# One stage's routing weights brought to the partitions by DMA instead of by matmul

## The reference, cut to what matters

```python
logits = jnp.einsum('bsd,de->bse', xn, Wr) + br
top_vals, top_idx = jax.lax.top_k(logits, K)                 # K = 2 of E = 8
w = jax.nn.softmax(top_vals, axis=-1)
w_full = jnp.einsum('bsk,bske->bse', w, jax.nn.one_hot(top_idx, E, dtype=w.dtype))
for e in range(E):
    h = jax.nn.gelu(jnp.einsum('bsd,dh->bsh', xn, W1[e]) + b1[e], approximate=False)   # H = 128
    y_e = jnp.einsum('bsh,hd->bsd', h, W2[e]) + b2[e]
    y = y + y_e * w_full[..., e, None]
```

## Time and profile before

| | |
|---|---|
| median of 3 runs | 560.65 us (560.37 to 564.43) |
| the profiled execution | 558.65 us |
| its span, first to last instruction | 556.9 us |
| TensorE busy | 515.6 us, 93% |
| VectorE busy | 458.4 us, 82% |
| ScalarE busy | 353.8 us, 64% |
| GpSimd busy | 80.0 us, 14% |
| expert units | from 464.9 us to the end |

### The profile page before, as it was taken

The page is one execution under the profiler, slowest core; times in us unless marked ns, Lnnn a source line. Parts: engine busy times, 40 slices in busy tenths (PEclk is TensorE's granted clock), DMA queues, the critical chain, the costliest instruction groups (busy, mean ns, idle before and its releaser), DMA issues.

```text
span 556.9 us, 12956 instructions
## 1 busy us (share of the span) xinstructions
PE 515.6 (93%) x4238; PEld 176.7 (32%) x4238; DVE 458.4 (82%) x540; ACT 353.8 (64%) x625; POOL 80.0 (14%) x180
## 2 busy tenths in 40 slices
PE   7999898557999999999999999999999888999996
PEld 6233332221333333333333333333333343233221
DVE  2668687778999999999999999999999786766644
ACT  2011222323889889898898898988988766445442
POOL 9601010203010010100100101001000451111000
PEclk9999999865999999999999999999999999999999
DMA  7910369373233232232332322323234101000000
GB/s 267 237 33 2 89 197 258 86 212 97 56 88 80 58 93 76 74 82 65 86 80 60 87 74 82 78 61 89 77 96 113 53 11 32 22 9 12 19 20 19
DMA packets 51095, 46.33 MB, mean 83 GB/s; under 512 B 26265, under 2 KB 39034, under 8 KB 51066
## 3 DMA queue, kind: packets, MB, share of 16 engines
q1 hardware_dynamic: 51066, 45.94, 30.5%
HBM read 29.75 MB, written 16.17 MB: 82 GB/s over the span
## 4 chain that ended last, share of the span: by engine, by line
PE 67%; DVE 5%; issue 1%; DMA 1%; ACT 1%; SPq 1%; POOL 0%; DVEq 0%; ACTq 0%; POOLq 0%
PE ps L1400 24%; PE ps L1312 13%; PE ps L1385 13%; PE ps L1533 5%; PE ps L1559 5%; DVE nmax L869 2%; PE ps L1326 1%; PE ps L1389 1%; DVE probs L1144 1%; PE ps L1546 1%; SPq L408 1%; PE ps L1450 1%; DMA maxima<-max_t 1%; PE ps L1556 1%; PE ps L1437 0%
## 5 line engine op out<-in xcount | busy, mean ns | idle before, releaser
L869 DVE TENSOR_REDUCE nmax<-ps 128x1 f32<-128x1024 f32 x256 | 301.6, 1218 | 18.7 <-PE ps L1312 9.9
L724 ACT ACTIVATE probs<-ps 128x512 f32<-128x512 f32 x512 | 278.1, 596 | 56.0 <-PE ps L1385 46.0
L1400 PE MATMUL ps<-probs,v_ring 128*32 128x256 f32 x2048 | 164.1, 393 | 0.0
L1312 PE MATMUL ps<-k_ring,q_ring 48*128 48x512 bf16 x512 | 102.9, 399 | 6.9 <-DVE nmax L869 6.9
L1385 PE MATMUL ps<-q_ring,k_ring 51*128 51x512 bf16 x512 | 101.3, 384 | 5.9 <-DMA q_ring<-maxima 1.7
L1312 PEld LDWEIGHTS ps<-k_ring,q_ring 48*128 48x128 bf16 x512 | 24.8, 93 | 113.7 <-issue 98.8
L1400 PEld LDWEIGHTS ps<-probs,v_ring 128*32 128x32 f32 x2048 | 40.5, 108 | 61.7 <-issue 36.8
L1144 DVE TENSOR_TENSOR probs<-probs,ps 128x1024 f32<-128x1024 f32 x32 | 39.0, 1220 | 25.4 <-PE ps L1546 20.1
L743 ACT ACTIVATE probs<-ps,wide_w 128x1024 f32<-128x1024 f32 x32 | 35.3, 1114 | 35.0 <-PE ps L1533 33.2
L890 DVE SCALAR_TENSOR_TENSOR gated<-ps,v_s,gamma_sb 128x1024 f32<-128x1024 f32 x32 | 40.7, 1280 | 10.9 <-PE ps L1234 10.7
L577 POOL TENSOR_TENSOR max_p<-nmax,zeros 128x8 bf16<-128x8 f32 x32 | 6.5, 202 | 282.4 <-DVE nmax L869 259.3
(11 more groups left out here) (162 smaller groups left out, 327.6 us busy)
## 6 DMA issues: line engine op xcount, KB each, us to landing
k_ring<-qk_parts SPq DMA_DIRECT2D x64, 96.0 KB, 2.4
q_ring<-qk_parts SPq DMA_DIRECT2D x64, 96.0 KB, 2.4
gamma_sb<-gamma_t SPq DMA_DIRECT2D x4, 1024.0 KB, 10.2
v_padded<-v_pad SPq DMA_DIRECT2D x4, 1024.0 KB, 5.0
v_ring<-v_padded SPq DMA_DIRECT2D x32, 128.0 KB, 3.2
outputs<-o_t SPq DMA_DIRECT2D x32, 128.0 KB
qk_parts<-qk_h SPq DMA_DIRECT2D x8, 384.0 KB, 4.3
x_ring<-bias_parts SPq DMA_DIRECT2D x32, 96.0 KB, 3.1
```

The lines of the kernel that those rows point to most:

```text
L724: A.activation(probs[:, s % 4, HALF * j:HALF * (j + 1)], ps[:, key_bank(s, j), :], ACT.Exp).then_inc(exp_done[j], 1)
L869: V.tensor_reduce(nmax[:, par, s:s + 1], ps[:, bank:bank + 2, :].rearrange("p a n -> p (a n)"), AX, ALU.max, negate=True).then_inc(s1_redu ...
L1312: return mm(ps[:, bank + j, :], q_ring[rows, u, P * s:P * (s + 1)], k_ring[rows, u, HALF * j:HALF * (j + 1)], start=True, stop=(s > 0 or j ...
L1400: last = mm(ps[VC * j:VC * (j + 1), PVB, 0:2 * P], v_ring[:, u, m, :], probs[:, m % 4, 2 * P * j:2 * P * (j + 1)], start=(m == 0), stop=(m ...
```

## The change

The weights of the units in `SENT` are no longer spread by TensorE. `SENT` is every unit k with k % 4 not zero and k above 2: units 3, 5, 6, 7, 9, 10, 11, 13 and so on to 31. That makes 22 of the 32 units as the code stands (24 have k % 4 not zero; units 1 and 2 are left out).

VectorE turns each batch's `w_full` in blocks of 32 x 32 (`weight_rows`, one transpose of 128 x 64 fp32 for each batch). SyncE stores the result in a DRAM tensor as one row of 128 weights for each tile and expert (`store_weights`: four DMAs a batch, of 64 runs of 128 bytes each). For each sent unit it loads them, the same four rows to each of the 128 partitions (`load_weights`: two DMAs, each 128 x 4 runs of 512 bytes, 256 KB, together 512 KB), into one of two buffers `w_wide`. The load into a buffer waits until the multiplication two sent units earlier has read it. The multiplication of a sent unit takes `w_wide` instead of the PSUM banks, and no longer waits for `spread`.

```diff
+    SENT = tuple(k for k in range(UNITS) if k % (E // 2) and k > 2)
...
+    w_scratch = nc.dram_tensor("weight_rows", [B, NT * E, P], fp32).ap()
...
+        w_rows = sb("w_rows", [P, B, NT * E], fp32)
+        w_wide = gated
...
+            def store_weights(b):
+
+                sp.wait_ge(w_rows_ready, b + 1)
+                for q in range(4):
+                    rows = slice(VC * q, VC * (q + 1))
+                    sp.dma_start(w_scratch[b, :, rows].rearrange("(h r) t -> r h t", h=2),
+                                 w_rows[rows, b, :].rearrange("r (h t) -> r h t", h=2)).then_inc(w_stored[b], 16)
+
+            def load_weights(k):
+
+                i, b, e = SENT.index(k), k // E, k % E
+                if i >= 2:
+                    sp.wait_ge(hid_scaled, SENT[i - 2] + 1)
+                sp.wait_ge(w_stored[b], 16 * 4)
+                for j in range(2):
+                    of = w_scratch[b, E * j + e, :]
+                    sp.dma_start(w_wide[:, i % 2, HALF * j:HALF * (j + 1)].rearrange("p (c n) -> p c n", n=P),
+                                 bass.AP(tensor=of.tensor, offset=of.offset, ap=[[0, P], [2 * E * P, NT // 2], [1, P]])
+                                 ).then_inc(w_loaded[i % 2], 16)
+
+            store_weights(0)
             store_output(G // RING + 1, (RING - 1) % 2, G - 1, RING - 1)
             for i in range(2):
                 sp.wait_ge(o_stored[i], 16 * G // 2 + 1)
             load_sums(B - 1)
+            for k in SENT[0:2]:
+                load_weights(k)
             store_inverse(B - 1)
             load_inverse(B - 1)
...
+            for k in SENT[2:]:
+                if k == E + 1:
+                    for b in range(1, B - 1):
+                        store_weights(b)
+                load_weights(k)
+                if k == 2 * E + 3:
+                    store_weights(B - 1)
+                if k > E and k % E == 5:
+                    store_result(k // E - 1)
+            store_result(B - 1)
...
+            def weight_rows(b):
+                V.transpose(w_rows[:, b, :], w_full[:, NT * b:NT * (b + 1), :].rearrange("p m e -> p (m e)")
+                            ).then_inc(w_rows_ready, 1)
...
-                               (weights_copy, 0), (first_choice, 1), (second_top, 1)):
+                               (weight_rows, 0), (weights_copy, 0), (first_choice, 1), (second_top, 1)):
...
-            WITHIN = {0: [(second_choice, 1)], 2: [(invert_sums, B - 1)], 4: [(two_weights, 1)], 5: [(all_weights, 1)],
+            WITHIN = {0: [(second_choice, 1)], 2: [(invert_sums, B - 1)], 4: [(two_weights, 1)], 5: [(all_weights, 1), (weight_rows, 1), (weight_rows, 2)],
...
-                dve.wait_ge(spread_done, k + 1)
                 if k >= 2:
                     dve.wait_ge(down_done, k - 1)
-                V.tensor_tensor(hid_w[:, k % 2, :], hid[:, k % 2, :],
-                                ps[:, 4:6, :].rearrange("p a n -> p (a n)"), ALU.mult).then_inc(hid_scaled, 1)
+                if k in SENT:
+                    i = SENT.index(k)
+                    dve.wait_ge(w_loaded[i % 2], 16 * 2 * (i // 2 + 1))
+                    weights = w_wide[:, i % 2, :]
+                else:
+                    dve.wait_ge(spread_done, spread_before(k) + 1)
+                    weights = ps[:, 4:6, :].rearrange("p a n -> p (a n)")
+                V.tensor_tensor(hid_w[:, k % 2, :], hid[:, k % 2, :], weights, ALU.mult).then_inc(hid_scaled, 1)
...
-                    pe.wait_ge(hid_scaled, k)
+                    pe.wait_ge(hid_scaled, max(n for n in range(k) if n not in SENT) + 1)
...
-                spread(k)
+                if k not in SENT:
+                    spread(k)
```

More of the change, by code:

```diff
@@ L288, in vit_tower_kernel @@
         y_seq = sem("y_seq")
+        w_rows_ready = sem("w_rows_ready")
+        w_stored = [sem(f"w_stored{b}") for b in range(B)]
+        w_loaded = [sem(f"w_loaded{i}") for i in range(2)]
         out_stored = [sem(f"out_stored{i}") for i in range(2)]
@@ L311, in up_bank, with spread_before @@
             return 0 if k % 2 else 2
+        def spread_before(k):
+            return k - sum(n < k for n in SENT)
         block = ctx.enter_context(nc.Block())
@@ L482, in _, with store_result @@
             load_sums(B - 1)
+            for k in SENT[0:2]:
+                load_weights(k)
             store_inverse(B - 1)
             load_inverse(B - 1)
-            for b in range(B):
+            def store_result(b):
                 halves = 2 if b == B - 1 else 1
@@ L1131, in residual @@
                 V.tensor_tensor(out_h, ye_v, h_v, ALU.add).then_inc(out_ready, 1)
-            WITHIN = {0: [(second_choice, 1)], 2: [(invert_sums, B - 1)], 4: [(two_weights, 1)], 5: [(all_weights, 1)],
+            WITHIN = {0: [(second_choice, 1)], 2: [(invert_sums, B - 1)], 4: [(two_weights, 1)], 5: [(all_weights, 1), (weight_rows, 1), (weight_rows, 2)],
                       6: [(route_parts, 1)], E: [(add_residual, B - 1), (center, B - 1)], E + 1: [(variance, B - 1)],
                       E + 2: [(scale, B - 1)], E + 6: [(logits_bias, B - 1), (first_choice, 2)],
-                      E + 7: [(second_top, 2), (second_choice, 2)], 2 * E + 1: [(two_weights, 2), (all_weights, 2)],
+                      E + 7: [(second_top, 2), (second_choice, 2)], 2 * E + 1: [(two_weights, 2), (all_weights, 2), (weight_rows, B - 1)],
                       2 * E + 2: [(route_parts, 2)]}
```

## The result

| | before | changed |
|---|---|---|
| median | 562.54 us (4 runs) | 617.99 us (4 runs, 613.66 to 620.43) |
| span of the profiled execution | 556.9 us | 615.1 us |
| first multiplication to end of span | 87.7 us | 142.7 us |

The ratio is 1.097, with a 95% interval of 1.092 to 1.103: the change made the kernel 9.7% slower. Nearly all of it arises in the expert units. The first multiplication (VectorE's product of `hid` and the weights, unit 0) starts at 469.25 us before and at 472.38 us after; from there to the end it is 556.9 - 469.25 = 87.7 us before and 615.1 - 472.38 = 142.7 us after, 55.1 of the 58.2 us by which the spans differ.

The account below looks back on a forecast made before the run. TensorE, full in the expert units, was taken as the bound: -0.4 - 3.96 - 0.6 + 0.3 = -4.66, say -4.6 us, from a median of 560.65 to 556.0 us; full range 554.0 to 577 us.

Parts of the forecast that it names:

- The bound, and the price of a pair: Expert units: TensorE is full, and each removed pair of spreading matmuls gives its queue back 0.22 us, 22 pairs 4.84 us.
- Transposes and stores: Four VectorE transposes at 0.25 us each, up to 0.5, and the stores on SyncE: hidden, at double price 0.5 us more.
- The cover of the sums: Sums, loaded later behind the first stores, land at 473.5 us; VectorE uses them at 475.18 us: 1.7 us of cover.
- The loads in steady state: Expert units: a load's data take up to 2.65 us, within the 2.83 us allowed; two buffers fit with nothing over.
- rival A: Loads run at the pace of `x_ring`, 264 packets a microsecond, 3.9 us each: 574.8 us on the median; chance 0.32.
- The first load: Unit 3's load, issued at about 473.4 us behind sums and outputs, expected at 477.6 us: cost 0.3 us.
- SyncE's queue: After the new stores, behind the first loads' four issues ending by 475.9 us, later transfers keep their cover: cost 0.
- It hardly moves: The store of the inverse sums, behind the issues of the first two loads on SyncE, was to stay nearly in place.
- Rival B: The round trip of the two buffers binds: at 5.0 us from multiplication's end to landing, 562.7 us; chance 0.15.
- The clock: Granted clock stays 1.00; if slow loads give TensorE gaps, it may be granted at the lower level, adding time.
- The range: 554.0 to 577 us, including slow loads at 3.9 us each; their slower half, chance some 0.16, stays outside.

Follow-up runs that it names:

- pairs_only: Changed kernel without transposes, stores or loads of weights, so the 22 pairs of spreading matmuls are gone with nothing in their place: 557.63 us, 0.994 of the kernel before.
- early_loads: rows2k_4buf with the load of unit 6 also issued ahead of the store and load of the inverse sums: 560.04 us, 0.994 of the kernel before.
- no_loads: Changed kernel with its transposes and stores but without the loads of weights and the waits for them: 559.42 us, 0.996 of the kernel before.
- same_4buf: Changed kernel with four buffers for the spread weights instead of two: 597.04 us, 1.061 of the kernel before.
- distinct: Changed kernel with each partition loading rows of its own from the input mixing matrix, same runs and buffers: 565.87 us, 1.003 of the kernel before.
- spaced: Changed kernel with transpose columns reordered and weights stored so a load's four shared rows lie 1 KB apart: 572.78 us, 1.019 of the kernel before.
- rows2k_4buf: rows2k with four buffers, one DMA a load and the first load issued before the wait for the last head's output: 563.15 us, 1.001 of the kernel before.
- copies: rows2k with each batch's rows stored 16 times, each eight partitions reading a copy of their own: 572.94 us, 1.017 of the kernel before.
- rows2k: Changed kernel with columns ordered before the transpose, so a load's four rows are one run of 2 KB: 568.62 us, 1.013 of the kernel before.

## Why the prediction was wrong

- **The bound, and the price of a pair: right.** TensorE was the bound, and 22 pairs less brought 3.7 us of stretch in *pairs_only* against 5.0 us forecast for it. In *early_loads* a unit is what the sum said: from 518 to 546 us TensorE was busy 27.63 of 28 us, and its chain runs at 1.06 + 1.01 = 2.07 us a unit:

```profile
529.63 1.06 PE ps L1588 x4
530.69 1.01 PE ps L1614 x4
```

- **Transposes and stores: right.** The transposes took 232 ns each, 250 forecast from the earlier trace rows, and with the stores cost 0.2 us of stretch (*no_loads*).

```profile
L1153 DVE STREAM_TRANSPOSE w_rows<-w_full 128x64 f32<-128x64 f32 x4 | 0.9, 232 | 0.1
```

- **The cover of the sums: right.** VectorE inverted the sums at 478.36 us, right behind the multiplication of unit 2, without waiting for them.
- **"The loads in steady state": the step that failed, and with it the result.** The prediction took a load at 2.65 us or less, from stores that read and write distinct addresses, against the one row of the profile that shows a load of the same kind, and left that choice open. A load took 5.7 us, and 4.8 us with four buffers (*same_4buf*). Even rival A, with 0.32 the second likeliest, was nearly half again too quick: 264 packets a microsecond against 1,024 / 5.7 = 180. `x_ring`'s rows lie 512 bytes apart; how fast shared rows are read depends on how they lie, and this step had no term for that. A's mechanism (the reading of a few shared rows holds engines that are idle between packets) is what the runs show, and its reason, aligned pieces of 256 bytes by the Trainium skill (*DMA: Bandwidth & Descriptors*, How a descriptor splits into AXI transactions), is not: *distinct* and *spaced* read the same number of pieces as the changed kernel, at 454 and 324 packets a microsecond.
- **The first load, and SyncE's queue behind it: wrong by some 2 and 3.6 us even with fast loads.** The first load was put at 0.3 us, issued at about 473.4 us. It was issued at 475.91 us in the changed kernel, whose unit 3 waited 7.89 us, and at 477.17 us in *distinct*, whose unit 3 waited 2.10 us with fast loads; in *rows2k_4buf*, where it goes at 472.55 us, that wait is gone. The four issues of the first two loads, put at 2.4 us, took 4.31 us in the changed kernel and 2.63 in *distinct*. "It hardly moves" was said of the inverse sums. The chain of the changed kernel shows otherwise: their store needed 9.04 us from issue to landing, behind the loads (of before, the pair of load and use is the earlier trace rows), and the load for unit 6 was issued only at 490.65 us, behind them. With loads that are fast this is what remained: units 5 to 6 are 5.7 us apart in *rows2k_4buf* and 2.1 in *pairs_only*. One load moved ahead gave 88.22 - 85.85 = 2.4 us of stretch back.
- **Rival B: real, but small where loads are fast.** With 2.3 us of data two buffers did not suffice: *distinct* waited 13.7 us in eight multiplications, six of them behind unit 6. Four buffers left two waits of 5.2 us in all, yet gave only 0.6 us of stretch. With the slow loads of the change, four buffers gave 16.7 us of its 55.1, by keeping the queue fuller.
- **The clock: right in direction.** With gaps in TensorE the granted clock fell to 0.85, and the same matmuls of `up` and `down` took 83.3 us of TensorE's time instead of 71.0. How much of these 12.3 us lengthened the kernel was not separated from the waits they run beside.
- **The range** ended at 577 us, at rival A's lower price. The text had a price of 7.9 us, 647 us, and left it out as the slower half of A. The result lay between the two.

The version that came out of this, *early_loads*, computes what the reference does and is 0.6% faster than the kernel before (0.989 to 0.998). *pairs_only* gives the same 0.6%, with 1.9 us less of stretch. *early_loads* needs runs of 2 KB, four buffers, one DMA a load and its place in SyncE's order, to remove matmuls worth 0.22 us each.

## What to carry to other kernels

A load that gives the same few rows of DRAM to all partitions has to be priced by a row of that kind and of that spacing, never by the rate of loads or stores of distinct addresses; look at the share of the DMA engines beside the rate, since engines that are idle between packets say that something else sets the pace. Before concluding on a cause from one fast variant, hold everything but one thing: here the variant with distinct rows changed the spacing too, and only its control showed which of the two had mattered. Look into the trace of a variant that "did nothing", too: *copies* read faster, and its stores hid that. And a transfer that replaces on-chip work needs its issue looked at as well: what it queues behind on an in-order engine, and how long its buffer's round is.

## What the runs showed of the hardware

- All partitions reading one 512-byte row, or four of them 8 KB apart, went at 71 to 108 packets a microsecond at the start of a load, engines 18 to 39% busy, in an input tensor and in one written just before; four rows 1 KB apart went at 324 in the stored tensor and at 460 in the input tensor, and rows of each partition's own, 1 KB apart, at 454 to 478.
- Runs of 2 KB read by all partitions came at 82 to 115 packets a microsecond (*rows2k*, 521 to 524 and 514 to 518 us, engines 74 to 95% busy), little above the pace of the slow 512-byte ones. So the slow start looks like a limit on reads and not on bytes; that is a reading of these rows, not a test of its own.
- The 32 KB store of the inverse sums landed 2.9 us after its issue in the kernel before, 4.4 us in *distinct* and 9.0 us in the changed kernel, behind the slow loads.
- The slow pace of 512-byte rows lasted some 5 us from the start of a load, then the same rows came at over 400 packets a microsecond. What ends it is open: no run here moved only the spacing in steps, gave each partition rows of its own 8 KB apart, or let the engines start apart. That the rows fall on the same part of the memory is argued from the spacing, not shown.
- An fp32 multiplication of 128 x 1024 took 1,225 ns with both operands in SBUF and 1,218 with one in PSUM.
- The part ahead of the expert units, the same in all kernels, ended between 469 and 480 us in the profiled executions; the medians carry that, and effects of 1% were read from the stretch behind it as well.
